# Layer norm and row store of the next block, moved into the chunk attention's pipeline

## The reference, cut to what matters

```python
h = _layernorm(x, axis=-1) * (1 + ca) + sa
x = x + ga * _L0_attn_ref(h, ...)
h = _layernorm(x, axis=-1) * (1 + cb) + sb
x = x + gb * _L0_ffn_ref(h, ...)        # the six-layer block

def _layernorm(x, axis=-1, eps=1e-05):
    m = jnp.mean(x, axis=axis, keepdims=True)
    v = jnp.var(x, axis=axis, keepdims=True)
    return (x - m) / jnp.sqrt(v + eps)
```

```python
scores = jnp.einsum('bhid,bhjd->bhij', qi, ki) * scale
attn = jax.nn.softmax(jnp.where(mask, -jnp.inf, scores), axis=-1)
chunk_out = jnp.einsum('bhij,bhjd->bhid', attn, vi) + 0.1 * jnp.einsum('bhid,bhde->bhie', qi, M)
```

## Time and profile before

| | |
|---|---|
| median of 3 runs | 5337.85 us (5337.22 to 5338.35) |
| the profiled execution, its own time | 5338.09 us |
| span of its core | 5336.1 us |
| mean granted TensorE clock | 0.953 |
| PE busy | 4702.5 us (88%) |
| DVE busy | 3901.9 us (73%) |
| ACT busy | 3192.5 us (60%) |
| POOL busy | 2748.3 us (52%) |

### The profile page before, as it was taken

The page is one execution under the profiler, slowest core; times in us unless marked ns, Lnnn a source line. Parts: engine busy times, 40 slices in busy tenths (PEclk is TensorE's granted clock), DMA queues, the critical chain, the costliest instruction groups (busy, mean ns, idle before and its releaser), DMA issues. The chain is left out here.

```text
span 5336.1 us, 215539 instructions
## 1 busy us (share of the span) xinstructions
PE 4702.5 (88%) x79056; PEld 3400.8 (64%) x79056; DVE 3901.9 (73%) x8390; ACT 3192.5 (60%) x6716; POOL 2748.3 (52%) x3885
## 2 busy tenths in 40 slices
PE   3568949999999999999999999999998566999996
PEld 2556736676767676667676676767666444666665
DVE  5984567777777777777777777777775856777775
ACT  1002526667777676776766777767676334677775
POOL 0004126666666666666666666666664324555552
PEclk6997979999999999999999999999999688999998
DMA  1000125555545454545454545455543003444442
GB/s 61 12 1 21 41 68 133 135 131 136 134 133 133 133 131 131 135 124 143 127 141 127 142 129 138 128 138 129 138 129 91 10 7 89 112 111 111 114 111 78
DMA packets 708752, 564.99 MB, mean 106 GB/s; under 512 B 227460, under 2 KB 633704, under 8 KB 707848
## 3 DMA queue, kind: packets, MB, share of 16 engines
q1 hardware_dynamic: 694920, 538.05, 38.1%
q10 hardware_dynamic: 13312, 22.02, 1.3%
HBM read 360.07 MB, written 200.02 MB: 105 GB/s over the span
## 5 line engine op out<-in xcount | busy, mean ns | idle before, releaser
L2110 POOL TENSOR_TENSOR L_qk<-L_cos_part,L_sin_part 128x512 f32<-128x512 f32 x896 | 1129.3, 1275 | 168.5 <-DVE L_sin_part L1995 168.2
L1780 ACT ACTIVATE L_squares<-L_ps_q 128x512 f32<-128x512 f32 x896 | 535.0, 597 | 975.2 <-PE L_ps_q L1532 968.9
L1532 PE MATMUL L_ps_q<-L_w_qkv,L_xT 128*128 128x512 f32 x1792 | 970.6, 624 | 23.0 <-DVE L_sin_part L1995 11.7
L2101 POOL TENSOR_TENSOR L_qk<-L_qk,L_rnorm 128x1024 f32<-128x1024 f32 (+1 forms) x512 | 865.1, 1690 | 20.3 <-POOL L_rnorm L2091 0.5
L1567 PEld LDWEIGHTS L_ps_t<-L_ident,L_qk 128*128 128x128 f32 x3584 | 446.2, 141 | 475.4 <-issue 373.7
L1994 DVE TENSOR_TENSOR L_cos_part<-L_ps_q,L_rot 128x512 f32<-128x512 f32 x896 | 609.5, 680 | 40.3 <-POOL L_rot L2120 35.0
L1995 DVE TENSOR_TENSOR L_sin_part<-L_ps_q,L_rot 128x512 f32<-128x512 f32 x896 | 609.7, 680 | 0.0
L1996 DVE TENSOR_REDUCE L_sumsq<-L_squares 128x8 f32<-128x512 f32 x896 | 605.3, 676 | 0.0
L2085 POOL TENSOR_TENSOR L_nw_a<-L_rnorm 128x32 f32<-128x32 f32 (+1 forms) x256 | 60.0, 234 | 1016.5 <-ACT L_rnorm L1810 1016.4
L1567 PE MATMUL L_ps_t<-L_ident,L_qk 128*128 128x128 f32 x3584 | 539.4, 273 | 2.6 <-POOL L_qk L2101 1.8
L1791 ACT ACTIVATE L_qkT<-L_ps_t 128x512 f32<-128x512 f32 x896 | 530.0, 591 | 13.5 <-PE L_ps_t L1567 13.5
(11 more groups left out here) (289 smaller groups left out, 9012.6 us busy)
## 6 DMA issues: line engine op xcount, KB each, us to landing
L_val<-v_rows SPq DMA_DIRECT2D x896, 260.0 KB, 3.9
v_rows<-L_val SPq DMA_DIRECT2D x384, 260.0 KB, 2.1
v_rows<-L_val SPq DMA_DIRECT2D x512, 65.0 KB, 2.0
L_rot_base<-in_rot SPq DMA_DIRECT2D x256, 128.0 KB, 2.1
v_rows<-L_val SPq DMA_DIRECT2D x128, 130.0 KB, 2.1
L_x_in<-x_rows SPq DMA_DIRECT2D x512, 32.0 KB, 1.7
mid_rows<-z SPq DMA_DIRECT2D x256, 64.0 KB, 1.6
L_f_in<-mid_rows SPq DMA_DIRECT2D x256, 64.0 KB, 2.0
```

Of the source, the lines that this page charges most:

```text
L1532: nc.tensor.matmul(ps_q[j % 2][:, :], xT[:, parity(t), :], w_qkv[:, 0:2, 256 * j:256 * j + 256], start=True, stop=True).then_inc(S["proj_p ...
L1780: nc.scalar.activation(squares[:, j % 2, :], ps_q[j % 2][:, :], ACT.Square).then_inc(S["sq_done"], 1)
L2101: nc.gpsimd.tensor_tensor(v, v, r, ALU.mult).then_inc(S["normed"], 1)
L2110: nc.gpsimd.tensor_tensor(qk[:, t % 2, h, s, :], cos_part[:, j % 2, :], sin_part[:, j % 2, :], ALU.add).then_inc(S["added"], 1)
```

## The change

`feed_stage` is no longer called. Its work moves into the loops of the attention's pipeline, four tiles (a group g) at a time. DVE gets `next_norm(i)` at the end of each iteration: the statistics of tile i-3, and for each group the small chain of the inverse root in two portions, six instructions in the iteration of the group's last tile and seven in the one after it. ACT normalises two tiles in each of two iterations (8 and 9 after the group's first). POOL multiplies and adds (`modulate(g)`) in its iteration 4g + 12, and SP stores (`store_rows(g)`) in its iteration 4g + 14.

```diff
@@ SP
+                    def store_rows(g):
+                        sp.wait_ge(S["z_done"], g + 1)
+                        r = 512 * g + g // 4 + 1
+                        sp.dma_start(x_rows[r:r + 512, :].rearrange("(t p) d -> p t d", p=128), z[:, 4 * g:4 * g + 4, :]).then_inc(rows_out[g % 2], 16)
...
+                        if i >= 14 and (i - 14) % 4 == 0:
+                            store_rows((i - 14) // 4)
+                    for g in range((TILES + LAST - 15) // 4 + 1, GROUPS):
+                        store_rows(g)
@@ POOL
+                    def modulate(g):
+                        zg = z[:, 4 * g:4 * g + 4, :]
+                        vec = lambda n: mods[:, g // 4:g // 4 + 1, n, :].to_broadcast([128, 4, 128])
+                        pool.wait_ge(S["ln_done"], g + 1)
+                        nc.gpsimd.tensor_tensor(zg, zg, vec(4), ALU.mult).then_inc(S["z_mul"], 1)
+                        pool.wait_ge(S["z_mul"], g + 1)
+                        nc.gpsimd.tensor_tensor(zg, zg, vec(3), ALU.add).then_inc(S["z_done"], 1)
...
+                        if i >= 12 and (i - 12) % 4 == 0:
+                            modulate((i - 12) // 4)
+                    for g in range((TILES + 2 - 13) // 4 + 1, GROUPS):
+                        modulate(g)
@@ ACT
-                    for i in range(TILES + LAST):
-                        emit(i)
+                    def next_norm(i):
+                        g, part = (i - 8) // 4, (i - 8) % 4
+                        if 0 <= g < GROUPS and part < 2:
+                            act.wait_ge(S["ln_roots"], g + 1)
+                            for j in (2 * part, 2 * part + 1):
+                                last = nc.scalar.activation(z[:, 4 * g + j, :], xr[:, 4 * g + j, :], ACT.Identity, bias=n_shift[:, g, j:j + 1], scale=n_rstd[:, g, j:j + 1])
+                            if part == 1:
+                                last.then_inc(S["ln_done"], 1)
+                    for i in range(TILES + 6):
+                        if i < TILES + LAST:
+                            emit(i)
+                        next_norm(i)
@@ DVE
+                    def newton(g):
+                        r = n_rstd[:, g, :]
+                        step(nc.vector.tensor_tensor(n_tmp[:, :], r, r, ALU.mult))
+                        step(nc.vector.tensor_tensor(n_tmp[:, :], n_tmp[:, :], n_half[:, :], ALU.mult))
+                        step(nc.vector.scalar_tensor_tensor(r, n_tmp[:, :], 1.5, r, ALU.add, ALU.mult))
+                    def next_norm(i):
+                        t = i - 3
+                        if live(t):
+                            dve.wait_ge(S["x_done"], t + 1)
+                            step(nc.vector.bn_stats(n_st[:, :], xr[:, t, :]))
+                            step(nc.vector.bn_aggr(n_mv[:, (t // 4) % 2, t % 4, :], n_st[:, :]))
+                        if live(t) and t % 4 == 3:
+                            g = t // 4
+                            step(nc.vector.tensor_scalar(n_var[:, :], n_mv[:, g % 2, :, 1], LN_EPS, None, ALU.add))
+                            step(nc.vector.tensor_scalar(n_rstd[:, g, :].bitcast(I32), n_var[:, :].bitcast(I32), -0.5, 1597463007.0, ALU.mult, ALU.add))
+                            step(nc.vector.tensor_scalar(n_half[:, :], n_var[:, :], -0.5, None, ALU.mult))
+                            newton(g)
+                        if live(t - 1) and t % 4 == 0:
+                            g = (t - 1) // 4
+                            newton(g)
+                            newton(g)
+                            nc.vector.scalar_tensor_tensor(n_shift[:, g, :], n_mv[:, g % 2, :, 0], -1.0, n_rstd[:, g, :], ALU.mult, ALU.mult).then_inc(S["ln_roots"], 1)
+                            dve.wait_ge(S["ln_roots"], g + 1)
-                    for i in range(TILES + LAST):
+                    for i in range(TILES + LAST + 1):
                         normalise(i)
                         residual(i)
                         shift(i)
+                        next_norm(i)
@@ two_layer_kernel
-        feed_stage(nc, "feed0", xr, mods, 0, z, x_rows)
```

More of the change, by code:

```diff
@@ L161, in _, with delta_attention_stage @@
                         step(nc.vector.scalar_tensor_tensor(out[:, 2, :], sign[:, :], -1.0, mag[:, :], ALU.add, ALU.mult))
-def delta_attention_stage(nc, x_dram, xr, mods, w_qkvT, w_oT, alpha_raw, beta_raw, tables, qkv_dram):
+def delta_attention_stage(nc, x_dram, xr, mods, w_qkvT, w_oT, alpha_raw, beta_raw, tables, qkv_dram, z, x_rows):
     H, DH, SUB, N_SUB = 16, 8, 32, 128
@@ L449, in delta_attention_stage @@
                 "qT_done", "kT_done", "attq_done", "pT_done", "exped",
-                "rec_done", "scaled", "att_done", "x_done", "max_done", "shifted")}
-            qk_loaded, v_loaded = [S["qk_in0"], S["qk_in1"]], [S["v_in0"], S["v_in1"]]
+                "rec_done", "scaled", "att_done", "x_done", "max_done", "shifted",
+                "ln_steps", "ln_roots", "ln_done", "z_mul", "z_done", "rows_out0", "rows_out1")}
+            qk_loaded, v_loaded, rows_out = [S["qk_in0"], S["qk_in1"]], [S["v_in0"], S["v_in1"]], [S["rows_out0"], S["rows_out1"]]
+            n_st, n_mv = sb("n_st", [128, 6]), sb("n_mv", [128, 2, 4, 2])
+            n_var, n_half, n_tmp = (sb(f"n_{n}", [128, 4]) for n in ("var", "half", "tmp"))
+            n_rstd, n_shift = sb("n_rstd", [128, TILES // 4, 4]), sb("n_shift", [128, TILES // 4, 4])
+            GROUPS = TILES // 4
             TURN, LAST = 4, 3
@@ L504, in _ @@
                                              qkv_dram[2][t * 128:t * 128 + 128, :].rearrange("(c k) d -> k c d", c=2)).then_inc(v_loaded[t % 2], 16)
+                        if i >= 14 and (i - 14) % 4 == 0:
+                            store_rows((i - 14) // 4)
+                    for g in range((TILES + LAST - 15) // 4 + 1, GROUPS):
+                        store_rows(g)
+                    for j in range(2):
+                        sp.wait_ge(rows_out[j], 16 * GROUPS // 2)
                 @block.gpsimd
                 def _(pool):
+                    def modulate(g):
[5 more added lines that the diff above has]
+                        nc.gpsimd.tensor_tensor(zg, zg, vec(3), ALU.add).then_inc(S["z_done"], 1)
                     pool.wait_ge(S["zeroed"], 2)
@@ L711, in _ @@
                         nc.vector.tensor_tensor(w_og[:, b, :], w_o[:, :], mods[:, b, 2, :], ALU.mult).then_inc(S["gated"], 1)
-                    for i in range(TILES + LAST):
+                    step = Steps(dve, S["ln_steps"])
+                    def newton(g):
[22 more added lines that the diff above has]
+                    for i in range(TILES + LAST + 1):
                         normalise(i)
@@ L2170, in two_layer_kernel @@
         delta_attention_stage(nc, t["L0_attn_x"], xr, mods, [t["L0_attn_WqT"], t["L0_attn_WkT"], t["L0_attn_WvT"]], t["L0_attn_WoT"],
-                              t["L0_attn_alpha_raw"], t["L0_attn_beta_raw"], t, qkv)
-        feed_stage(nc, "feed0", xr, mods, 0, z, x_rows)
+                              t["L0_attn_alpha_raw"], t["L0_attn_beta_raw"], t, qkv, z, x_rows)
         names = dict(qkv="Wqkv", out="Wo", w1="W1", w2="W2", b1="b1", b2="b2", ln_g="ln_g", ln_b="ln_b", q_scale="q_scale", k_scale="k_scale")
```

## The result

| | before | changed |
|---|---|---|
| median | 5338.09 us (15 runs, 5335.42 to 5340.94) | 5353.49 us (15 runs, 5345.84 to 5360.44) |
| the profiled execution | 5338.09 us, span 5336.1 | 5345.84 us, span 5344.1 |
| mean granted clock | 0.953 | 0.951 |

The ratio is 1.0028, 95% interval 1.0021 to 1.0036: slower by 15 us. The forecast was 5346, no change, with a range of 5325 to 5357. The changed kernel's times spread over 14.6 us, the old one's over 5.5; its profiled execution is the shortest of the 15.

The account below looks back on a forecast made before the run. Whatever delays DVE's reciprocal delays the whole attention round, with 0.50 us of slack: 5338.1 - 29.9 (stage's end) + 30.3 (added in rounds) + 8 (clock) = 5346 us, no change within 0.2% (5327.2 to 5348.5); range 5325 to 5357.

Parts of the forecast that it names:

- The end of the stage: From the last residual to the six-layer block's first DMA: 40.5 us become 10.6 us, 29.9 us saved.
- both kernels pay that: From the last store's issue to the next stage, landing and barrier: 3.18 us, the same in both kernels.
- Rounds 3 of four: DVE's statistics pair and seven small instructions before the reciprocal: 1.38 us late, 7 times, 9.7 us.
- Rounds 2 of four: Pair and six small DVE instructions: 1.2 us late once; held by POOL's passes, 3.1 us late six times, 18.6 us.
- POOL's plain copy: POOL's 0.40 us mem_t copy might hold a DVE instruction in rounds 2 and 3: up to 3.5 us, left out.
- ACT, the pair of statistics, the store: ACT's activations 0.6 us late, 0.8 us with the statistics pair's excess; the store costs nothing.
- The sum of the added work: All lateness added inside the attention rounds: 9.7 + 1.2 + 18.6 + 0.8 = 30.3 us.
- The clock: TensorE's stalls lower its granted clock about seven times at 1.1 us: 8 us, bounds 0 to 15 us.
- Rival E: POOL holds DVE six times as forecast, but no clock is lost: 5338.5 us, 7%.
- Rival B: The 1.4 us stalls also take the clock, in more than nine rounds, and POOL's copy holds an instruction: 5355 us, 22%.
- C: POOL's passes and DVE's small instructions don't meet: 18.9 us added, clock 0 to 4 us, 5327 to 5331 us, 14%.
- D: TensorE works meanwhile, so half of the reciprocal's delay is absorbed: 5325 us, down to 5315, 7%.

Follow-up runs that it names:

- fill_eight_on: Changed kernel with 14 and 6 extra TensorE matmuls filling the stalls of rounds 2 and 3 of four, from round 8 on: 5347.91 us, ratio 1.0017.
- pool_late: Changed kernel with POOL's two passes and the row store two iterations later: 5338.62 us, ratio 1.0.
- dve_alone: Kernel before plus DVE's `next_norm` alone, its results unused and `feed_stage` kept: 5370.03 us, ratio 1.0062.
- dve_and_pool: Kernel before plus DVE's `next_norm` and POOL's two passes on scratch, without ACT's normalisation and the store: 5388.18 us, ratio 1.0097.
- after_again: Changed kernel again, unaltered, for a second profile and more times: median 5352.86 us, ratio 1.0024.
- after_third: Changed kernel a third time, unaltered, for its profile alone: a single execution of 5350.34 us.
- chain_early: Changed kernel with DVE's `next_norm` of the iteration before placed between normalise and residual instead of behind the shift: 5314.60 us, ratio 0.9953.
- fill_fitted: Changed kernel with 14 and 6 extra TensorE matmuls in the stalls, fills in rounds 3 to 8 included: 5349.68 us, ratio 1.0022.
- fill_stalls: Changed kernel with 22 and 10 extra TensorE matmuls placed in the stalls that rounds 2 and 3 of four cause: 5366.64 us, ratio 1.0058.

## Why the prediction was right, and where it was short

- **The end of the stage.** Forecast 29.9 us, measured 29.0. From the residual's end to the next stage it is 11.55 us for 10.6. The chain is as forecast (n_shift 2.95 us after the residual's end, against 2.87). What is short is the step "both kernels pay that" for 3.18 us: from the end of POOL's second pass (753.42), behind which the store is issued, to the next stage are 4.09 us. SP's wait for the landing of the store ends 2.31 us after its issue in both kernels (755.76 and 748.76); the difference lies behind it, where POOL clears the semaphores of the stage that ends (L53). That takes 0.40 us for the attention stage's 68 in the changed kernel, with a drain of 0.30 us ahead of it, and 0.05 with 0.06 us for the four of `feed_stage`. The old kernel clears the attention stage's too (0.37 us), between the last residual and `feed_stage`, inside the 40.5 us. So the short exit went and the long one stayed, and my sum had it the other way round. The three clearings, the first in the changed kernel:

```profile
L53 POOLq EVENT_SEMAPHORE_RANGE_CLEAR  x1: 395/395/395, 756.8 to 756.8; - x1
```

```profile
L53 POOLq EVENT_SEMAPHORE_RANGE_CLEAR  x1: 369/369/369, 709.5 to 709.5; - x1
...
L53 POOLq EVENT_SEMAPHORE_RANGE_CLEAR  x1: 49/49/49, 749.3 to 749.3; - x1
```

- **Rounds 3 of four.** Forecast 1.38 us each, measured 8.21 - 6.76 = 1.45 at the full clock (fill_eight_on, pool_late, dve_alone alike).
- **Rounds 2 of four.** Forecast 3.1 us each, measured 3.25. Which instructions are held was off by one place (the third tensor_scalar and the second Newton step, not the first Newton step and the third): the copy had made the second tensor_scalar longer, so the third started 1.00 us after the shift's end instead of 0.90, just behind POOL's pass (0.90 against 0.93). The end is the same, since the end of POOL's second pass sets it. Without the meeting a round 2 costs 1.28 us (dve_alone, pool_late), near the bound of 1.19.
- **POOL's plain copy.** The row left it open, and the rule of the Trainium skill (GPSIMD Engine Reference, § specifications) made no exception for it. The rule is right in kind: a tensor_scalar took 0.31 us beside the copy of the changed kernel, 0.38 in dve_alone, instead of 0.17. By it the sum would have been up to 3.5 us higher; the steps are longer than forecast by 0.15 us in rounds 2 and 0.07 us in rounds 3, so that the copy can have added 6 x 0.15 + 7 x 0.07 = 1.4 us at most.
- **ACT, the pair of statistics, the store.** Forecast 0.8 us, measured 1.4 with the clock held. The other rounds take 0.06 us more each, and as much in dve_and_pool, without ACT and store. Round 13 alone takes 0.4 us more (7.17 us in both fitted fills, in after_again and in after_third, 6.80 in dve_and_pool), so ACT or the store may cost something there once; no run tells which.
- **The sum of the added work.** Forecast 30.3 us, measured 31.7 with the clock held (fill_eight_on): 20.3 in rounds 2, 9.9 in rounds 3, 1.4 in the others.
- **The clock.** Forecast seven falls at 1.1 us, 8 us. In the first profile there are seven falls before the drain, 7.6 us. But the two other profiles have 12.3 and 5.7 us. Seven falls stand in each of the three, but the engine was at the lower level for 51, 68 and 37 us in them, by windows of 0.5 us, where seven times 3.5 us would be 24.5. So the count was right, the length was not, and an us at the lower level cost 0.15 to 0.18 us instead of 0.31. Why it cost less was not tried; TensorE was busy for nearly all of it (10.38 of 10.50 us from 557 on), so its slower work probably filled waits that the same rounds have at the full clock. The two errors cancelled in the mean (8.6): the size of this term was right by luck. The spread stands in no term of mine: the fall of 14 us in after_again took 4.3 us (2.77 and 1.50 over the old rounds). Rival E (no loss) is excluded. Rival B's condition, falls in more than nine rounds, was not met in number; the slower end came by longer falls instead. pool_late shows that B's mechanism exists: there the clock fell behind pairs of stalls of 1.58 and 1.76 us, and at 526 us behind a single one of 1.58.
- **What I left out.** That the stages behind are not of constant length. I added the change of the span to the old profile's time as if they were. In the three profiles of the changed kernel they took 4589.1 us in the mean, 2.7 more than in the two of the old one. 31.7 + 8.6 - 29.0 + 2.7 = 14.0 us; the profiles' mean spans differ by 13.8 us, the medians by 15.4 and 14.5. The six-layer block has no part in it: from its first load to that of the linear block it took 3393.4 us in the mean of either kernel. The block of two layers has: from its first load to the first store of the output are 879.6, 883.8 and 883.7 us in the three profiles, 880.0 and 881.0 in the two. But over all 14 profiles that stretch is 879.5 to 884.6 us, and dve_alone, which keeps `feed_stage`, has the longest, pool_late the shortest. So nothing shows that the change makes it longer; five profiles can't tell that from chance, and it stays open.
- **C and D.** C (no meeting) has not happened in this kernel; pool_late makes it happen, but for one meeting, and came out at 5338.6 us against the 5327 to 5331 of that case. In its profile the reciprocal falls back by 27.1 us from round 4 to 32, 8.2 more than C's 18.9. The meeting before reciprocal 32 is 2.0 of it, and the steps of 1.28 and 1.45 us, seven of each, where C has 1.2 and 1.38, are 1.0. That leaves some 5 us, most of it the clock's, against 0 to 4 that C allowed for it: the clock fell in every group, where I had thought that the shorter stalls would mostly spare it. D (lateness absorbed) is excluded: the step of the reciprocal is longer by all of the delay (3.25 us in rounds 2).

The mistake worth keeping is in the balance, not in a term: 30 against 30 with a clock term of one sign. The mechanism held, and differences of one sign (1.4 us of added work, 0.9 us at the stage's end, 0.6 us of clock, 2.7 us behind) carried the time out of "no change". A sum like that should have said "slower" with more than 38%.

## What to carry to other kernels

Ask of each idle stretch of an engine who waits for what follows it: the 0.50 us before the reciprocal were in everybody's way and the 1.5 us before the residual in no one's, and the same chain delays the reciprocal by 39 us in the one place (26 us of it without POOL's passes, dve_alone) and by nothing in the other. Small DVE instructions that read only SBUF should not be placed where POOL starts a long pass over SBUF, above all not where one event releases both. A stall on TensorE's path should be priced with the clock that it may cost in the round behind it.

## What the runs showed of the hardware

- POOL's tensor_tensor of 1.26 us holds a DVE instruction of four columns from its start to POOL's end: 0.16 becomes 1.11 to 1.20 us. The next DVE instruction then goes through in 0.16 us even as POOL's next pass starts, and the one after is held again. It hits tensor_scalar (one input) as well as tensor_tensor. A plain copy on POOL of 0.40 us does the same to a smaller amount (0.16 to 0.17 becomes 0.25 to 0.39 us).
- bn_stats and bn_aggr keep their 0.28 and 0.18 us beside POOL's passes (seven of each in chain_early), and DVE instructions that read PSUM keep their times as well (the residual's 0.29 us, five times in pool_late).
- The changed kernel's times spread more than the old one's: 14.6 us over 15 runs and 13.8 over 11, against 5.5 over 15, 9.3 over 15, 8.3 over 19 and 9.5 over 21. That its falling clock is the reason is not shown: with the clock held in the pipeline the spread was 6.3 us over 9 runs (fill_fitted), 10.1 over 11 (fill_eight_on) and 17.3 over 5 (fill_stalls), and with falls 11.8 over 11 (pool_late).
- A 128-column fp32 matmul behind others takes 0.23 us, its two records together. Filling a stall exactly is hard: with eight and four matmuls too many (fill_stalls, 5366.64 us) it cost more than the clock that it kept.
- From the last store's issue to the next stage's first load are 3.18 us behind `feed_stage`, 3.50 behind the linear block and 4.06 behind the changed attention stage. POOL's clearing of the stage's semaphores took 0.05, 0.31 and 0.40 us of them.
